# Rounding in a quantised feed-forward stage moved from VectorE to ScalarE, with a second buffer of gated rows and the loop written out

## What is computed

```
x_norm = rmsnorm(layernorm(h), g_in)                    # per row
scale  = 127 / max(|x_norm|, 1e-5)                      # per row
x_q    = clip(round(x_norm * scale), -128, 127) / scale
w_q    = clip(round(w * s), -1, 1) / s                  # s = 1 / mean(|w|)
up, gate = split(x_q @ w_in_q.T, 2)                     # 2 x 512 columns
y      = silu(gate) * up
y_q    = the same rounding of rmsnorm(y, g_out)         # rows of 512
out    = h + y_q @ w_out_q.T
```

## Time and profile before

| | us |
|---|---|
| median of 3 runs | 3263.02 |
| lowest, highest | 3258.48, 3264.15 |
| the profiled execution | 3261.98 |
| its span, first to last instruction | 3260.1 |
| the layer that is changed, from its first statistics to the end of the span | 2739.5 to 3260.1 |

### The profile page before, as it was taken

The page is one execution under the profiler, slowest core; times in us unless marked ns, Lnnn a source line. Parts: engine busy times, 40 slices in busy tenths (PEclk is TensorE's granted clock), DMA queues, the critical chain, the costliest instruction groups (busy, mean ns, idle before and its releaser), DMA issues. The chain is left out here.

```text
span 3260.1 us, 47434 instructions
## 1 busy us (share of the span) xinstructions
PE 2635.0 (81%) x13374; PEld 1932.9 (59%) x13375; DVE 2267.7 (70%) x5978; ACT 1367.3 (42%) x2304; POOL 913.1 (28%) x943
## 2 busy tenths in 40 slices
PE   7999999999979999966664899926767775777655
PEld 3555555555548888855553899925555664444333
DVE  5777777777748989865554444446576665999997
ACT  2333333333323333333332566635454351555555
POOL 2001001000000000026665344466464430333332
PEclk9999999999989999965555899966677686555666
DMA  1000000000000000022223677721111100000000
GB/s 55 1 0 26 0 0 26 0 0 0 0 7 0 0 0 0 0 99 79 80 80 111 226 256 260 257 80 43 30 43 30 34 22 19 13 21 21 21 17 25
DMA packets 67222, 161.79 MB, mean 50 GB/s; under 512 B 12974, under 2 KB 30562, under 8 KB 66402
## 3 DMA queue, kind: packets, MB, share of 16 engines
q1 hardware_dynamic: 37578, 94.18, 8.9%
q0 software_dynamic: 21504, 44.99, 4.8%
q10 hardware_dynamic: 8064, 21.68, 2.2%
HBM read 63.89 MB, written 63.88 MB: 39 GB/s over the span
## 5 line engine op out<-in xcount | busy, mean ns | idle before, releaser
L353 DVE TENSOR_REDUCE pmax<-ppre 112x1 f32<-112x448 f32 x784 | 477.8, 623 | 129.0 <-PE ppre L211 126.9
L173 ACT ACTIVATE prob<-pscore 128x896 f32<-128x896 f32 x336 | 305.5, 917 | 589.2 <-PE pscore L243 492.1
L255 PE MATMUL pout<-prob,xkey 128*64 128x448 f32 x1344 | 327.1, 565 | 0.2 <-ACT prob L173 0.2
L211 PE MATMUL ppre<-xhl,yh 113*112 113x448 f32 x784 | 317.5, 406 | 6.6 <-DVE pmax L353 5.1
L211 PEld LDWEIGHTS ppre<-xhl,yh 113*112 113x112 f32 x784 | 138.3, 177 | 214.5 <-DVE pmax L353 153.1
L242 PE MATMUL pscore<-yh,xhl 113*128 113x448 f32 x644 | 242.2, 376 | 0.0
L1042 POOL DMA_INDIRECT rows_in<-xn,idx x224 | 217.5, 971 | 66.1 <-issue 62.7
L1622 POOL DMA_INDIRECT yg<-rows_out,place x224 | 218.4, 975 | 62.5 <-issue 62.2
L243 PE MATMUL pscore<-yl,xhl 113*128 113x448 f32 x644 | 235.6, 366 | 0.0
L2074 POOL TENSOR_TENSOR yg<-y,gout 112x512 f32<-112x512 f32 x112 | 142.1, 1269 | 229.2 <-DVE y L2307 224.7
L1480 POOL TENSOR_TENSOR zl<-z,zh 128x448 fp32r<-128x448 f32 x126 | 144.5, 1147 | 212.2 <-ACT zh L1453 202.8
(11 more groups left out here) (372 smaller groups left out, 6649.3 us busy)
## 6 DMA issues: line engine op xcount, KB each, us to landing
wd<-down SPq DMA_DIRECT2D x63, 512.0 KB, 3.0
xb<-rows_in SPq DMA_DIRECT2D x63, 448.0 KB, 3.6
rows_out<-yb ACTq DMA_DIRECT2D x63, 336.0 KB, 3.2
out<-ho SPq DMA_DIRECT2D x28, 336.0 KB, 2.8
rows_in<-zero SPq DMA_DIRECT2D x15, 448.0 KB, 5.3
x<-in_xT SPq DMA_DIRECT2D x8, 600.2 KB
rows_in<-xn,idx POOLq DMA_INDIRECT x224, 2.6
yg<-rows_out,place POOLq DMA_INDIRECT x224
```

What stands on the lines that cost most here:

```text
L173: nc.scalar.activation(prob[j % 3][:, :, :], pscore[j % 2][:, :, 0:CH], ACT.Exp).then_inc(exped, 1)
L211: pe.matmul(ppre[k % 2][:, 0:CH], yh1[:, q * T:(q + 1) * T], xhl[b % 2][:, kc * CH:(kc + 1) * CH], start=True, stop=True).then_inc(pre_mm, 1)
L255: mm = pe.matmul(pout[i * LO:(i + 1) * LO, 0:CH], xkey[b % 2][:, 2 * j + i, :], prob[j % 3][:, i, :], start=(j == 0), stop=(i == 1 and j = ...
L353: nc.vector.reduce_max(pmax[:, q, kc:kc + 1], ppre[k % 2][:, 0:CH], AX.X).then_inc(pre_max, 1)
```

## The change

VectorE no longer rounds. It stops at the scales: `quant_in` ends with `sx` and signals `sx_out`; `quant_y` ends with `s2` and signals `s2_out`. ScalarE gets two new functions: `round_x` (four activations of 112x192 with the scale of each row, a wait for its own result, one activation of 112x768 to bf16) and `round_y` (four activations of 112x512 with the scale of each row). The copy of `r2` to `s2` (L2332) goes.

On ScalarE `round_y(g-1)` stands first in the step, `round_x(g+1)` stands behind `take_y(g-1)`, and the squares of tile 3 move behind `take_x(g+1)`. `yg` has two buffers, so that GpSimd can write group g while ScalarE still rounds g-1. The loops of all engines are written out in Python, with constants in the waits. TensorE's order of work is the same.

```diff
@@ buffers
-        yg = sb("yg5", [T, TPC, HID])
+        yg = [sb(f"yg5_{i}", [T, TPC, HID]) for i in range(2)]
@@ gpsimd, chunk
                         pool.wait_ge(S["r2_out"], g)
-                        pool.wait_ge(S["yr_out"], g)
+                        if g >= 2:
+                            pool.wait_ge(S["yr_out"], 2 * g - 2)
...
@@ sync, gpsimd, tensor, scalar, vector: the loop, here ScalarE's
-            with act.Fori(1, NC - 1) as g:
+            for g in range(1, NC - 1):
                 step(g)
@@ scalar
+            def round_x(g):
+
+                act.wait_ge(S["sx_out"], g + 1)
+                for q in range(TPC):
+                    rx = nc.scalar.activation(xr[:, q, :], xg[:, q, :], ACT.Copy, bias=MAGIC, scale=sx[:, q:q + 1])
+                rx.then_inc(S["xr_out"], 1)
+                act.wait_ge(S["xr_out"], g + 1)
+                nc.scalar.activation(xq[:], xr[:], ACT.Copy, bias=-MAGIC).then_inc(S["xq_out"], 1)
+
+            def round_y(g):
+
+                act.wait_ge(S["s2_out"], g + 1)
+                for q in range(TPC):
+                    ry = nc.scalar.activation(yr[:, q, :], yg[g % 2][:, q, :], ACT.Copy, bias=MAGIC, scale=s2[:, q:q + 1])
+                    if q % 2:
+                        ry.then_inc(S["yr_out"], 1)
...
             def step(g, first=False, last=False):
                 if not first:
+                    round_y(g - 1)
                     whole_y(g - 1, 0)
...
                 if not first:
                     take_y(g - 1)
-                for q in (2, 3):
-                    squares(g, q)
+                if not last:
+                    round_x(g + 1)
+                squares(g, 2)
                 if not last:
                     take_x(g + 1)
+                squares(g, 3)
+                if not last:
                     silu(g + 1, 0)
                     silu(g + 1, 1)
@@ vector, weigh_in
+                if not isinstance(g, int) or g > 0:
+                    dve.wait_ge(S["xr_out"], g)
@@ vector, quant_in
-                link(nc.vector.tensor_tensor(sx[:], sx[:], fac[:, bass.ds(g * TPC, TPC)], ALU.mult))
-                for q in range(TPC):
-                    ins_ = nc.vector.tensor_scalar(xr[:, q, :], xg[:, q, :], sx[:, q:q + 1], MAGIC, ALU.mult, ALU.add)
-                ins_.then_inc(S["xr_out"], 1)
-                dve.wait_ge(S["xr_out"], g + 1)
-                nc.vector.tensor_scalar(xq[:], xr[:], MAGIC, None, ALU.subtract).then_inc(S["xq_out"], 1)
+                nc.vector.tensor_tensor(sx[:], sx[:], fac[:, bass.ds(g * TPC, TPC)], ALU.mult).then_inc(S["sx_out"], 1)
@@ vector, quant_y
-                link(nc.vector.tensor_copy(s2[:], r2[:]))
                 link(nc.vector.tensor_tensor(am2[:], am2[:], r2[:], ALU.mult))
...
-                link(nc.vector.tensor_tensor(s2[:], s2[:], r2[:], ALU.mult))
-                if not first:
-                    dve.wait_ge(S["yq_out"], 2 * g)
-                for q in range(TPC):
-                    ins_ = nc.vector.tensor_scalar(yr[:, q, :], yg[:, q, :], s2[:, q:q + 1], MAGIC, ALU.mult, ALU.add)
-                ins_.then_inc(S["yr_out"], 1)
+                nc.vector.tensor_tensor(s2[:], s2[:], r2[:], ALU.mult).then_inc(S["s2_out"], 1)
```

More of the change, by code:

```diff
@@ L2037, in bit_ffn_phase @@
                  "ssq_out", "r2_in", "r2_out", "gin_in", "yq_out", "ytr_mm", "yT_out", "o_mm", "o_out", "stored", "dvec",
-                 "dvec2", "fac_in", "fac_out", "poolc", "d2_out", "xr_out", "yr_out")
+                 "dvec2", "fac_in", "fac_out", "poolc", "d2_out", "xr_out", "yr_out", "sx_out", "s2_out")
         S = {n: sem(f"{n}_5") for n in names}
@@ L2052, in store @@
                 sp.dma_start(out_t[:, bass.ds(g * TPC, TPC), :], ho[:]).then_inc(S["stored"], 16)
-            with sp.Fori(0, NC) as g:
+            for g in range(NC):
                 store(g)
@@ L2073, in chunk @@
                     pool.wait_ge(S["y_out"], g * TPC + q + 1)
-                    nc.gpsimd.tensor_tensor(yg[:, q, :], y[:, q, :], gout[:], ALU.mult).then_inc(S["yg_out"], 1)
+                    nc.gpsimd.tensor_tensor(yg[g % 2][:, q, :], y[:, q, :], gout[:], ALU.mult).then_inc(S["yg_out"], 1)
                 pool.wait_ge(S["yg_out"], (g + 1) * TPC)
@@ L2079, in _ @@
             chunk(0, first=True)
-            with pool.Fori(1, NC) as g:
+            for g in range(1, NC):
                 chunk(g)
@@ L2153, in _ @@
             step(0, first=True)
-            with pe.Fori(1, NC - 1) as g:
+            for g in range(1, NC - 1):
                 step(g)
@@ L2210, in step @@
                     take_y(g - 1)
-                for q in (2, 3):
-                    squares(g, q)
+                if not last:
+                    round_x(g + 1)
+                squares(g, 2)
                 if not last:
                     take_x(g + 1)
+                squares(g, 3)
+                if not last:
                     silu(g + 1, 0)
                     silu(g + 1, 1)
+            round_x(0)
             take_x(0)
@@ L2221, in _ @@
             step(0, first=True)
-            with act.Fori(1, NC - 1) as g:
+            for g in range(1, NC - 1):
                 step(g)
             step(NC - 1, last=True)
+            round_y(NC - 1)
             whole_y(NC - 1, 0)
@@ L2230, in _ @@
         def _(dve):
-            L1, L2 = 6, 5
+            L1, L2 = 5, 4
             def weigh_in(g):
+                if not isinstance(g, int) or g > 0:
+                    dve.wait_ge(S["xr_out"], g)
                 for q in range(TPC):
@@ L2315, in largest_y @@
                 dve.wait_ge(S["yg_out"], g * TPC + 2 * pair + 2)
-                nc.vector.tensor_reduce(am2[:, 2 * pair:2 * pair + 2], yg[:, 2 * pair:2 * pair + 2, :], AX.X, ALU.max,
+                return nc.vector.tensor_reduce(am2[:, 2 * pair:2 * pair + 2], yg[g % 2][:, 2 * pair:2 * pair + 2, :], AX.X, ALU.max,
                                         apply_absolute_value=True)
             def quant_y(g, first=False):
-                st = [g * L2]
+                st = [g * L2 + 1]
                 def link(ins):
@@ L2325, in link @@
                     dve.wait_ge(S["dvec2"], st[0])
-                largest_y(g, 1)
+                largest_y(g, 1).then_inc(S["dvec2"], 1)
                 if not first:
                     result(g - 1, 1)
+                dve.wait_ge(S["dvec2"], g * L2 + 1)
+                dve.wait_ge(S["r2_in"], g + 1)
                 dve.wait_ge(S["r2_out"], g + 1)
-                dve.wait_ge(S["r2_in"], g + 1)
-                link(nc.vector.tensor_copy(s2[:], r2[:]))
                 link(nc.vector.tensor_tensor(am2[:], am2[:], r2[:], ALU.mult))
@@ L2336, in quant_y @@
                 link(nc.vector.tensor_scalar(am2[:], am2[:], 1e-5, 1.0 / 127, ALU.max, ALU.mult))
+                if not first:
+                    dve.wait_ge(S["yr_out"], 2 * g)
                 link(nc.vector.reciprocal(s2[:], am2[:]))
                 nc.vector.tensor_scalar(d2[:], am2[:], wsc[0:T, 1:2], None, ALU.mult).then_inc(S["d2_out"], 1)
-                link(nc.vector.tensor_tensor(s2[:], s2[:], r2[:], ALU.mult))
-                if not first:
-                    dve.wait_ge(S["yq_out"], 2 * g)
-                for q in range(TPC):
-                    ins_ = nc.vector.tensor_scalar(yr[:, q, :], yg[:, q, :], s2[:, q:q + 1], MAGIC, ALU.mult, ALU.add)
-                ins_.then_inc(S["yr_out"], 1)
+                nc.vector.tensor_tensor(s2[:], s2[:], r2[:], ALU.mult).then_inc(S["s2_out"], 1)
             def result(g, pair):
@@ L2376, in _ @@
             step(0, first=True)
-            with dve.Fori(1, NC - 1) as g:
+            for g in range(1, NC - 1):
                 step(g)
```

2 lines of the change are left out of this document (1 added, 1 removed).

## The result

| | before | changed |
|---|---|---|
| median us (4 executions each) | 3261.74 | 3337.57 |
| lowest, highest | 3258.48, 3264.15 | 3333.43, 3338.89 |
| ratio, 95% interval | | 1.0227, 1.0214 to 1.024 |
| profiled execution, span | 3261.98, 3260.1 | 3333.43, 3330.7 |

The change costs 2.3%. The forecast was 3338.

What follows compares the result with a forecast made beforehand. VectorE, busy 15.99 of 17.00 us, bounded the kernel; a 20.03 us turn, less 0.15 for the clock, meant 2.7 us more per group. 68 + 4 + 3.4 + 0.7 = 76 on 3262 gave 3338 us, range 3300 to 3362.

Steps and rivals of the forecast that it cites:

- (d): Squares of tile 3 behind the copy to `xT`, then `ms` and `ho` of the previous group: 1.54 us.
- (e): Once `po` is free: second `outof`, `into` of the next group, two `silu`, on to the next instruction: 5.60 us.
- The turn: From ScalarE's first rounding of `yr` to the next one, through five steps of waits: 20.03 us, against 17.17.
- (a): ScalarE from the first rounding of `yr` up to `round_x`: 8.47 us.
- Steady intervals: 25 intervals between groups, each 2.7 us longer: 68 us.
- First and last: First and last interval, which lack some of the instructions, 2 us each: 4 us.
- Group 0: Start of the layer: 0.9 us for slower input rounding, 2.5 for later mean squares: 3.4 us in the sum.
- Behind the last `ms`: End of the layer, behind the last group: rounding on ScalarE takes 0.7 us more.
- (c): Input transposes and copy, from the end of `xq` to the end of `xT`: 1.98 us.
- The clock up through the whole stretch: Rival: TensorE's clock is up in the critical stretch; fully fast, period 17.2 us, total 3270; half, 3302; chance 0.12.
- The relieved engine sets the pace: Rival: the chain has slack, VectorE's 13.3 and ScalarE's 14.6 us remain, period 14.6, total 3193; chance 0.07.
- Dearer links: Rival: roundings at upper bounds, `sx` late, instruction fetching; about 1 us more per group, total 3365; chance 0.10.

Runs made afterwards that it cites:

- e4: Kernel before with loops written out and, on VectorE, the previous group's result (tiles 0 and 1) ahead of the first maxima: period 16.26 us, ratio 0.9931.
- e2: Changed kernel with the previous group's result (tiles 0 and 1) ahead of the mean squares on VectorE: period 17.03 us, ratio 1.0012 to the kernel before.
- e1: Changed kernel with ScalarE's squares of tile 3 ahead of the copy to `xT` again: period 18.50 us, ratio 1.0119 to the kernel before.
- e8: Changed kernel with the edits of e1 and e2 together: period 17.05 us, ratio 1.0 to the kernel before.
- e3: Kernel before with the layer's five loops written out, nothing else: period 16.86 us, ratio 0.9984.
- e7: Changed kernel with input rounding on VectorE, half the gated-row rounding between the `silu`, squares ahead of `xT`, e4's VectorE order: 15.51 us, ratio 0.988.
- e5: Changed kernel with gated-row rounding back on VectorE and squares ahead of `xT`; only input rounding on ScalarE: period 17.82 us, ratio 1.005 to the kernel before.
- e10: Changed kernel with two of four gated-row tiles rounded between ScalarE's two `silu`: period 18.77 us, ratio 1.0136 to the kernel before.
- e9: Changed kernel with one buffer of gated rows instead of two: period 19.76 us, ratio 1.0211 to the kernel before.

## Why the prediction was right

**The bound and the chain.** The engine that was relieved did set the period (e4 takes away the one place where VectorE stood still, 0.60 us, and the period falls by as much), and its relief was worth nothing, because a chain of waits closed elsewhere and made the period 2.6 us longer. The deciding step was (d) with (e): the result that frees `po` stands behind the mean squares, these behind the last squares, and the change put those behind `xT`. e2 cuts this link on VectorE's side, e1 on ScalarE's, e8 shows that it is one link.

**The sizes.** The turn was 20.03 forecast and 19.91 measured. The roundings of the gated rows took 0.710 us each, 2.45 to the next instruction for four, where the forecast had 2.36 with 2.40 as its upper bound. The estimate by the Trainium skill (ScalarE: Activation LUTs, section What ACT_TABLE_LOAD costs), 0.706 and 2.45, was the better one. That step (a) came out at 8.44 all the same, against 8.47, is a cancelling: from the last `silu` of the step to `round_x` it took 3.53 us (3013.02 - 3009.49) where 3.62 was forecast. The input roundings took 0.451 against 0.43, and 1.49 for four as forecast. The ScalarE groups of the changed kernel:

```profile
L2202 ACT ACTIVATE yr<-yg,s 112x512 f32<-112x512 f32 x112 | 71.3, 710 | 4.4 <-DVE s L2362 4.4
...
L2193 ACT ACTIVATE xr<-xg,sx 112x192 f32<-112x192 f32 x112 | 41.8, 451 | 18.6 <-DVE sx L2322 18.6
L2171 ACT COPY xT<-pxt 96x896 bf16<-96x896 bf16 x28 | 25.2, 901 | 13.5 <-PE pxt L2098 13.5
L2196 ACT ACTIVATE xq<-xr 112x768 bf16<-112x768 f32 x28 | 23.6, 842 | 0.9
```

The margin of the scales `sx` was 0.30 us (3012.72 against 3013.02), where 0.1 was forecast: the forecast had L2293 held until GpSimd was done, and in the changed kernel the instruction in its place (L2319) gets through in 0.17 us and the next one is held, as in e3. It holds in the steady groups: the 18.6 us that ScalarE waited for `sx` are two waits, in groups 0 and 1 (16.5 and 2.1).

**The clock.** The forecast took 0.15 us off for a clock that rises mostly behind the products that count. The mean is 19.77 against 19.91 in an undisturbed turn, so 0.14. It comes in jumps: 20 intervals are 19.77 to 19.91, five 19.07 to 19.36. In one of the short ones the matmuls change to the 2.4 GHz level within the first two tiles (granted clock 0.50 from 2881 to 2884, 0.95 from 2884 to 2888):

```profile
2882.93 1.06 PE L2107 MATMUL pup<-winq,xT 96*112 96x512 bf16 x2
2883.78 0.88 PE L2107 MATMUL pga<-winq,xT 96*112 96x512 bf16 x2
2884.50 0.59 PE L2107 MATMUL pup<-winq,xT 96*112 96x512 bf16 x2
```

and the second `silu` comes 1.11 us behind the first instead of 1.71.

So the amount was right and the reason only in part. The prediction read the rise before the change as following work without a gap from 3021.04 to 3027.47, but TensorE stood idle for 1.03 us ahead of 3026.99 there. And gapless work did not bring the rise each time: from 3018.92 to 3027.45 of the changed kernel TensorE worked 8.5 us without a gap at a granted clock of 0.50, while in the turn ahead, which began at 2999.01 in the same way, the same pair of matmuls was already at the 2.4 GHz level. What decides it is open.

```profile
3004.36 0.59 PE L2107 MATMUL pup<-winq,xT 96*112 96x512 bf16 x2
...
3024.68 1.06 PE L2107 MATMUL pup<-winq,xT 96*112 96x512 bf16 x2
```

**The sum.** Steady intervals: 25 x (19.77 - 17.17) = 65, forecast 68. First and last: 17.11 - 15.25 and 16.43 - 14.71, 3.6 together, forecast 4. Group 0: its `ms` came at 2783.23 where it was at 2781.70, in a layer that began 1.44 us earlier, so 3.0, forecast 3.4. Behind the last `ms`: 19.75 against 19.1, 0.65, forecast 0.7. Sum 72.2 less the 1.4 of the earlier layers: 70.8, and the spans differ by 70.6. The medians differ by 75.8; the profiled execution of the changed kernel was the fastest of its four. The forecast of 3338 meets the median to half a microsecond, but its 76 us stand against 72.2 measured in the layer. That closeness is luck; the agreement within 4 us is not. (The bounds of -20 to +12 us that it names would give 3318 to 3350, and not the 3320 to 3356 that stands beside them. Nothing hangs on it here.)

**What it had wrong.** The loops written out were counted at nothing with a bound of 0.1 us per group. Where VectorE sets the period they are worth 0.31 (e3). This step looked at the durations of the small waits and instructions, and not at which of them GpSimd holds. By the trace it did not touch the sum, since in the changed kernel VectorE waits 2.7 us for ScalarE's `silu` and 4.2 for its squares.

VectorE was to be busy 13 us of a period and was busy 12.26. Most of the difference is again GpSimd: before, two of its weighings fell beside VectorE's four `xg`, which took 3.06 us; now one does, and they take 2.41. That had no effect on the period either.

**The rivals.** The clock up through the whole stretch: 0.65 granted on the mean of a turn, most of (c) to (e) at 1.06 us for two matmuls, so no. The relieved engine sets the pace: even with the worst link cut, 17.0 us remain (e2, e8), and of the kernels with a rounding on ScalarE only e7 is clearly below the kernel before. Dearer links: the roundings of `yr` were dearer by 0.09 us for four, but `sx` was in time, and written-out code shows no stall (e3 is faster than the loop, not slower), so no. The advice to move work off a saturated VectorE (Perfetto Trace Analysis, section Optimizing Scalar/DVE Operations, of the Trainium skill) thus holds in e7, at 0.988 where the order alone gives 0.9931 (e4), and not in the change, at 1.0227, with the same engine relieved.

What stays open: when the clock rises in a turn and when it doesn't, how e5's loss divides, and the changed kernel with its loops kept.

## What to carry to other kernels

Before moving work to an idle engine, write down the turn: from an instruction of one group to the same one of the next, through every wait; work put into the turn that sets the period costs its length however idle the engine is on the mean. Ask for each instruction that is moved who waits behind it on its engine, and let results that free a buffer stand ahead of instructions that wait for the moved work: one line of that kind was worth 2.7 us in 19.8. Idle time is worth something only where it stands: half of the rounding in a wait of 1.02 us took 1.0 us off the period (e10), against the whole of it behind the wait. And try the order of the work first: e4 gained 0.7% without moving any.

## What the runs showed of the hardware

Some of VectorE's instructions are held while GpSimd runs its 112x512 multiplication. L2293, on 112x4 numbers, takes 0.17 us where it starts 0.04 us ahead of it (e3) and 1.26 where it starts 0.02 behind (before), and with the shift of a few hundredths the hold goes from L2293 to the one behind it, worth 0.20 us per group in e3. The four `xg` are held as well: they take 3.06 us beside two weighings (before), 2.41 beside one (changed), and 1.40 in e9, where GpSimd starts its first weighing 2.7 us behind the start of `yr` instead of 0.6 ahead of it, and none falls beside them:

```profile
3038.25 1.40 DVE L2262 SCALAR_TENSOR_TENSOR xg<-h,mean,gin 112x192 f32<-112x192 f32 x4
```

Not all are held: in e9 GpSimd multiplies from 3040.06 to 3045.37, and the product at 3041.54 and the row maxima at 3042.21 take 0.75 and 0.94 us there, as they do elsewhere.

An activation of 112x512 with a scale from a tile in SBUF takes 0.710 us, and four of them follow each other at 0.61. The sums of squares, with constants, took 0.630 us before; they are another function with a sum beside it, so the 0.08 us between them is not shown to be the scale alone.
